# A DLRM tower on one core: handing over the x0b transfers one by one

## What is computed

```python
e = jnp.stack([tbl_0[ids[:, 0]], ..., tbl_31[ids[:, 31]]], axis=1)      # (1024, 32, 16)
xk = x0 = e
for W in (W0, W1, W2):                                                  # (32, h, 64)
    xk = relu(einsum('bmd,bhd,mhk->bkd', x0, xk, W))
    outs.append(sum(xk, axis=2))
h = concatenate(outs + [dense_ctx], axis=1)                             # (1024, 208)
h = relu(h @ W_top1 + b_top1); h = relu(h @ W_top2 + b_top2); y = h @ W_top3
```

## Time and profile before

| | |
|---|---|
| median of three runs | 791.03 us (784.43 to 791.82) |
| the profiled execution | 797.63 us |
| its span, first to last instruction | 795.8 us |
| mean granted TensorE clock in it | 0.953 |
| PE, DVE, POOL, ACT busy | 82%, 69%, 58%, 39% of the span |
| x0b: transfers, queue | 120 of 512 KB and 16 of 256 KB (block 0), SP |
| bytes moved | 121.57 MB, mean 153 GB/s |

### The profile page before, as it was taken

How to read it: one execution, slowest core, us unless ns; L and a number is a source line. 1 busy time by engine, 2 the same in 40 slices (tenths; PEclk the granted TensorE clock), 3 DMA queues, 4 the chain that set the end, 5 groups by cost and what they waited for, 6 DMA issues and landing times.

```text
span 795.8 us, 8373 instructions
## 1 busy us (share of the span) xinstructions
PE 656.4 (82%) x3096; PEld 268.9 (34%) x3096; DVE 551.6 (69%) x274; ACT 310.7 (39%) x586; POOL 464.6 (58%) x332
## 2 busy tenths in 40 slices
PE   0047798797989789897999799996988879999987
PEld 0012133233443334333443244433432334434435
DVE  1005796976939496796859496794939679798581
ACT  0004261616334171624535271714517072717131
POOL 6756687673838667358838667383956733335100
PEclk9999999898989899998999999899999999999998
DMA  7569749691983739663698749473793919872000
GB/s 182 125 185 229 207 137 212 177 208 37 259 237 72 147 116 224 183 144 75 183 205 212 141 139 229 156 160 58 212 229 100 199 46 255 216 168 45 0 1 0
DMA packets 59112, 121.57 MB, mean 153 GB/s; under 512 B 15369, under 2 KB 32017, under 8 KB 58977
## 3 DMA queue, kind: packets, MB, share of 16 engines
q1 hardware_dynamic: 40336, 112.41, 57.3%
q10 hardware_dynamic: 10544, 6.53, 2.8%
q0 software_dynamic: 8192, 2.11, 2.8%
HBM read 116.82 MB, written 5.25 MB: 153 GB/s over the span
## 4 chain that ended last, share of the span: by engine, by line
PE 47%; issue 15%; DVE 10%; ACT 9%; another core or an unknown queue 9%; POOL 9%; DMA 1%; DVEq 0%; ACTq 0%; POOLq 0%
PE acc L632 38%; DVE z_dve L373 9%; POOL emb L320 8%; ACT xq L449 4%; PE psm L701 3%; ACT xq L441 3%; PE psm L710 2%; PE acc L647 2%; ACT xs L441 1%; DMA emb<-in_tbl_dram,ids_cur 1%; PE psm L688 1%; POOL z_pool L329 1%; PE psm L678 1%; DVE zacc L398 0%
## 5 line engine op out<-in xcount | busy, mean ns | idle before, releaser
L373 DVE TENSOR_TENSOR z_dve<-xq,x0b 128x2048 f32<-128x2048 f32 x210 | 464.6, 2285 | 128.5 <-ACT xq L441 99.5
L632 PE MATMUL acc<-z_dve,w_cin 128*64 128x512 f32 x1680 | 393.5, 603 | 29.6 <-DVE z_dve L373 19.9
L329 POOL TENSOR_TENSOR z_pool<-x0b,xs 128x2048 f32<-128x2048 f32 x46 | 208.4, 4560 | 165.3 <-ACT xs L441 163.7
L320 POOL DMA_INDIRECT emb<-in_tbl_dram,ids_cur x256 | 246.7, 964 | 83.7 <-issue 80.2
L632 PEld LDWEIGHTS acc<-z_dve,w_cin 128*64 128x64 f32 x1680 | 119.6, 138 | 277.1 <-issue 206.4
L441 ACT ACTIVATE xq<-acc 64x512 f32<-64x512 f32 x128 | 73.0, 570 | 268.8 <-remote 151.7
L449 ACT ACTIVATE xq<-acc 32x512 f32<-32x512 f32 x256 | 144.4, 564 | 24.9 <-DVE z_dve L373 15.5
L373 DVE TENSOR_TENSOR z_dve<-xq,x_rot 128x2048 f32<-128x2048 f32 x30 | 68.0, 2292 | 41.1 <-PE acc L632 24.7
L632 PE MATMUL acc<-z_dve,w_sym 128*64 128x512 f32 x256 | 71.3, 639 | 19.0 <-issue 11.4
L632 PE MATMUL acc<-z_pool,w_cin 128*64 128x512 f32 x368 | 85.9, 602 | 0.0
L647 PE MATMUL acc<-z_extra,w_extra 128*64 128x128 f32 x256 | 31.0, 319 | 27.9 <-issue 25.7
(11 more groups left out here) (39 smaller groups left out, 188.6 us busy)
## 6 DMA issues: line engine op xcount, KB each, us to landing
x0b<-x0t SPq DMA_DIRECT2D x120, 512.0 KB
x_rot<-x0t SPq DMA_DIRECT2D x64, 512.0 KB
x_rep<-x0t SPq DMA_DIRECT2D x16, 512.0 KB
emb<-in_tbl_dram,ids_cur POOLq DMA_INDIRECT x256
x0b<-x0t SPq DMA_DIRECT2D x16, 256.0 KB
x0t<-emb_t ACTq DMA_DIRECT2D x14, 256.0 KB, 2.6
w_cin<-in_L_rec_W_dram SPq DMA_DIRECT2D x16, 64.0 KB
x_lo<-x0t SPq DMA_DIRECT2D x16, 64.0 KB
```

What stands on the lines that cost most here:

```text
L320: nc.gpsimd.indirect_dma_start(out=emb[:, D * f:D * f + D], out_offset=None, in_=tables[f], in_offset=bass.IndirectOffsetOnAxis(ap=ids_cur ...
L329: nc.gpsimd.tensor_tensor(z_pool[:, k % ZP_SLOTS, :, :], x0b[b % 2][:, 2 * j:2 * j + 2, :], xs[:, :].unsqueeze(1).broadcast_to([P, 2, N]), ...
L373: nc.vector.tensor_tensor(z_dve[:, k % Z_SLOTS, :, :], in0.unsqueeze(1).broadcast_to([P, 2, N]), in1, ALU.mult).then_inc(z_made, 1)
L632: ins = nc.tensor.matmul(acc[l][K * side:K * side + K, :], weights[c], z[:, c, NH * side:NH * side + NH], start=start and c == 0, stop=sto ...
```

## The change

The eight transfers of x0b(b+1) are no longer handed over together at the start of block b. The first four (first half) are issued one after the other, each behind a wait for one of the first four DVE products of L1(b). The last four (second half) stand behind `load_l0(b+2)` in SP's order, each behind a wait for one of the four NAT products of L2(b). Block 0's own loads, in groups of two chunks, stay as they were and only get a function of their own.

```diff
+            def load_x0b_group(g):
                 for r in range(4):
-                    sp.dma_start(x0b[b % 2][Q * r:Q * r + Q, c0:c1, :],
-                                 x0_rows(b, r + 4 * c0, [[0, Q], [4 * ROW, c1 - c0], [1, N]])
+                    sp.dma_start(x0b[0][Q * r:Q * r + Q, 2 * g:2 * g + 2, :],
+                                 x0_rows(0, r + 8 * g, [[0, Q], [4 * ROW, 2], [1, N]])
+                                 ).then_inc(x0b_in[0][g // 2], 16)
+
+            def load_x0b(b, c0, z_gates):
+
+                for r in range(4):
+                    sp.wait_ge(z_made, z_gates[r])
+                    sp.dma_start(x0b[b % 2][Q * r:Q * r + Q, c0:c0 + CH // 2, :],
+                                 x0_rows(b, r + 4 * c0, [[0, Q], [4 * ROW, CH // 2], [1, N]])
                                  ).then_inc(x0b_in[b % 2][c0 // (CH // 2)], 16)
...
-                load_x0b(0, 2 * g, 2 * g + 2)
+                load_x0b_group(g)
             for b in range(BLOCKS):
                 if b < LAST:
                     wait_x0t((b + 1) // 2)
                     if b > 0:
                         sp.wait_ge(z_made, l2_phase_end(b - 1, SWP))
                         sp.wait_ge(zp_made, zp_end(b - 1))
-                    load_x0b(b + 1, 0, CH // 2)
-                    load_x0b(b + 1, CH // 2, CH)
+                    load_x0b(b + 1, 0, [z_before[1, b, v, j] + 1 for v, j in l1_dve(b)[:4]])
...
                     sp.wait_ge(z_made, l0_end(b + 1))
                     sp.wait_ge(ze_made, b + 2)
                     load_l0(b + 2)
+                if b < LAST:
+                    load_x0b(b + 1, CH // 2, [z_before[2, b, NAT, j] + 1 for j in range(PAIRS)])
```

More of the change, by code:

```diff
@@ L248, in x0_rows @@
                 return bass.AP(x0t, t * (2 * M * ROW) + (row * ROW + s * N + col), dims)
-            def load_x0b(b, c0, c1):
+            def load_x0b_group(g):
                 for r in range(4):
-                    sp.dma_start(x0b[b % 2][Q * r:Q * r + Q, c0:c1, :],
-                                 x0_rows(b, r + 4 * c0, [[0, Q], [4 * ROW, c1 - c0], [1, N]])
+                    sp.dma_start(x0b[0][Q * r:Q * r + Q, 2 * g:2 * g + 2, :],
[6 more added lines that the diff above has]
+                                 x0_rows(b, r + 4 * c0, [[0, Q], [4 * ROW, CH // 2], [1, N]])
                                  ).then_inc(x0b_in[b % 2][c0 // (CH // 2)], 16)
```

## The result

| | before | after |
|---|---|---|
| median of four runs each | 791.42 us (784.43 to 796.93) | 899.09 us (895.82 to 899.92) |
| the profiled execution | 797.63 us | 895.82 us |
| its span | 795.8 us | 894.0 us |
| mean granted TensorE clock | 0.953 | 0.894 |

The changed kernel takes 1.135 times as long, with a 95% interval of 1.129 to 1.140. The forecast was 860 us, with a range of 828 to 888. The sign and the mechanism came as forecast, the size did not.

What follows compares the result with a forecast made beforehand. POOL's cycle (products, gathers, 2.8 us, ACT's copies) was taken as the bound. Six odd and five even blocks +62.0, then -4, +10.4 and +1: +69.4 on 797.63, 867.0 traced, 860.4 us as median, range 828 to 888.

Steps and rivals of the forecast that it cites:

- tile written after xs: Even blocks' `load_l0` waits for ACT's next tile, written 5.1 us after POOL begins the odd block's products.
- landing behind it: `load_l0` (12.5 us) and four late x0b transfers (10.1 us) land 22.6 us behind the written tile.
- third product to next xs: Odd blocks: POOL's third product 4.5, ids and gathers with z_extra 20.6, release 2.8, x1_pool 2.4 us.
- block 12: Even block after the summed eleven: 42 us in place of 46.0, so -4.
- block 13: Odd block without gathers: 5.1 + 22.6 + 4.5 + 8.8 for PE, then ACT's copies, 50.3 us, so +10.4.
- ahead of block 1: Block 0: `load_l0(1)` now stands behind four L1(0) products, put at 1 us (0 to 3).
- Rival A: 7%: PE's releases held from soon after the first gather; odd blocks 64.9 us, even blocks 46, about 926 us.
- B: 5%: DMA traffic holds PE and thinning it frees PE; even blocks 36.45 us, odd 50.3, about 781 us.
- C: 4%: the late half is absorbed, time within 1%, under 8 us in seven late blocks.
- the new even block: Even blocks with no late transfers: between 39.1 us (both ACT copies out of the chain) and 46.0, taken as 42.
- odd blocks, second half: Late x0b transfers issued in odd blocks, needed 9.1 us into POOL's next products: a few us of cover, cost nothing.
- the hold: PE's releases are held up while POOL issues gathers, and come out some 2.8 us behind the last one.

Runs made afterwards that it cites:

- waits alone: Kernel before with all eight waits, but the second half ahead of the tile's wait and of `load_l0`: 805.57 us, 1.011 of the kernel before.
- warm kernel: Changed kernel with twelve more 128x512 matmuls on PE in each odd block, after L1's third product: 846.25 us, 1.174 of the kernel before.
- the split: Kernel before with each block's second eight gathers held until PE releases L1(b): 744.09 us (0.923), then 740.39 (0.933) and 723.65 (1.007).

## Why the prediction was wrong, point by point

**The sum against the trace.** The traced time was to be 867.0 us and was 895.82. By the terms of the sum:

| term | forecast | measured | difference in all |
|---|---|---|---|
| tile written after xs, six odd blocks | 5.1 | 6.5 (5.1 to 8.8) | +8.6 |
| landing behind it | 22.6 | 23.3 (22.4 to 25.6) | +4.4 |
| third product to next xs | 30.3 | 30.4 | +0.4 |
| five even blocks, 2 to 10 | 42 | 44.1 (40.9 to 45.9) | +10.3 |
| block 12 | 42 | 46.7 | +4.7 |
| block 13 | 50.3 | 55.0 | +4.7 |
| ahead of block 1 (+1 forecast) and at the end | | | -4.3 |

That is +28.8 us, all of the miss of the traced time. The six even blocks are 15.0 of them. The median misses by 9.9 us more: I took off 6.6 us because the profiled execution of the kernel before was that much above its median, and the profiled one of after is 3.3 us below its own. That the offset would carry over was assumed.

**Right: what bounds, who waits, and where.** The third POOL product waits alone in blocks 1, 3, ... 13, for 18.4 to 24.5 us; the late transfers stand back to back behind `load_l0`; the odd blocks are 58 to 64 us; x2_nat and x2_swp run inside the burst there. The first half's waits cost nothing that can be told (waits alone, 1.011). Rival A's 65 us for the odd blocks didn't come (block 7's 64.2 us have a late tile and a landing of 25.6 us in them, and both copies ran inside the burst), nor B's 36 us for the even ones; C's absorption didn't either.

**The step that failed: the new even block.** It was put between 39.1 and 46.0 us, and I took 42, "nearer the middle", from no row; it measured 44.5 in the mean of six. With 42 in all six the median would have come out at 884 us, inside the range. Two things were left out of it, and the second is the larger.

Block 4 shows the first. Its 43.1 us are 9.1 of two products, 4.0 of waiting for x0b, 4.6 for the third, 20.2 from its end to the last gather's, and 5.2 to xs: the lower end of 39.1, plus the 4.0 us of a cover called sufficient in the part on odd blocks. The forecast costed "odd blocks, second half" at nothing and never asked what the even block would be with it. Block 12 has 0.9 us of this, the others none. Block 6's 44.6 us have another wait in them, 6.04 us behind POOL's first gather, which the kernel before has as well.

The second is the hold. In blocks 8, 10 and 12 (45.9, 45.9 and 46.7 us) no gain is left, and they are 12.4 of the 15.0 us. The changed kernel at the end of block 10, PE, POOL's last gather, ACT, and POOL's next products:

```profile
604.41 7.04 PE L641 MATMUL acc<-z_dve,w_cin 128*64 128x512 f32 x32
...
614.77 0.94 POOL L329 DMA_INDIRECT emb<-in_tbl_dram,ids_cur  x1 [0.31 <-issue]
...
618.34 2.31 ACT L450 ACTIVATE xq<-acc 64x512 f32<-64x512 f32 x4 [14.30 <-remote]
...
627.78 4.56 POOL L338 TENSOR_TENSOR z_pool<-x0b,xs 128x2048 f32<-128x2048 f32 x1 [12.06 <-ACT xs L450]
```

PE's L1 is over at 611.45 and x2_nat comes at 618.34, 6.9 us later and behind the last gather, with 12.06 us of POOL's idle time, as in the earlier trace rows. L1 ended 14 to 16 us into the burst in blocks 8, 10 and 12, and 11 us into it in blocks 2 and 4, which kept their gain. At the lower level, where nothing is held, blocks 2, 4, 8, 10 and 12 of the changed kernel all take 37.9 to 39.3 us. So in half of the even blocks it was rival A's even half that came, without its odd half. The two had been tied into one rival, though they are decided separately. Why L1 is later in blocks 8, 10 and 12 than in 2 and 4 stays open.

**A term mis-sized: the written tile.** 5.1 us was the interval of one pair of blocks. It was 5.1, 6.9, 8.8, 7.9, 5.5, 5.1 and 5.1 us in the seven. In block 4 ACT's last copy of the tile waited for PE:

```profile
312.02 0.59 ACT L529 COPY emb_t<-psm 128x512 f32<-128x512 f32 x1 [3.71 <-PE psm L687]
```

That the lateness of one pair is handed on to the next through PE is argued from this row, not shown by a run. The landing was sized nearly rightly from the rows, 23.3 us against 22.6. The fit of the Trainium skill ("SBUF — State Buffer", "The DMA setup-cost knee", with "Door 1: The DMA port swizzle"), which gave an estimate of 17.9 us, is further off; here the measurement decides.

**A term left out: PE's clock, in block 13.** The stretches of the changed kernel around block 5's gap (busy us of PE, PEld, DVE, ACT, POOL, then granted clock, DMA share, GB/s), and PE's rows there:

```profile
322.00:332.00 10.00, 9.61 (x42) 5.44 (x40) 0.85 (x1) 1.74 (x5) 0.00 (x0) 1.00 1.03 230
332.00:343.00 11.00, 0.00 (x0) 0.00 (x0) 4.35 (x2) 0.00 (x0) 4.30 (x1) 0.67 0.96 209
343.00:347.00 4.00, 3.74 (x10) 1.25 (x12) 4.00 (x4) 1.11 (x2) 3.12 (x5) 0.50 0.90 188
...
329.72 1.89 PE L641 MATMUL acc<-z_dve,w_cin 128*64 128x512 f32 x8
343.26 3.68 PE L641 MATMUL acc<-z_pool,w_cin 128*64 128x512 f32 x8 [11.65 <-POOL z_pool L338]
```

While PE stood for 11.65 us its granted clock fell from 1.00 to 0.50, from 2.4 to 1.2 GHz, and its next eight matmuls took 3.68 us in place of 1.89. The Trainium skill's page "TensorE: Matmul & The Clock Gate" (Part 1, on the clock gate) gives these two levels and says that an idle engine drops to the lower one; the trace agrees. In block 5 nobody waits for that: xs there hangs on the gathers. In block 13 there are none, PE's five products took 11.4 us and not 8.8, and that is some 2.6 of its 4.7 us (the landing's 24.5 us are another 1.9). The warm kernel says the same at the lower level. Its rows of PE in block 5, and then in block 15:

```profile
316.94 10.57 PE L758 MATMUL psm<-wt_a,ident 128*128 128x512 f32 x24
328.43 1.94 PE L642 MATMUL acc<-z_pool,w_cin 128*64 128x512 f32 x8 [0.92 <-POOL z_pool L339]
...
787.39 10.57 PE L758 MATMUL psm<-wt_a,ident 128*128 128x512 f32 x24
```

In block 5 PE is at full speed behind the gap. Yet the kernel's ratio of 1.174 (1.163 to 1.185) is no better than the unwarmed one's 1.167, and that is misleading: block 15 is odd too, but has no gap, and there the 10.57 us of extra matmuls stand in PE's way. From the start of block 15's products to the end the warm kernel takes 79.7 us, the unwarmed one 69.1. Up to there, from block 1 on, it takes 659.6 us against 661.3. So warming gained some 2 us in fourteen blocks, by one trace of each kernel; their runs spread by more (842 to 850 and 835 to 841 us). Block 13 is shorter, 51.4 against 54.3 us, and blocks 3, 5 and 7 by 1 to 3 us, but blocks 4 and 12 are 3 to 5 us longer.

**What the hold had to do with it.** At the lower level the changed kernel's chain is the same, only with nothing held. POOL in block 5 of the changed kernel there:

```profile
294.12 9.04 POOL L338 TENSOR_TENSOR z_pool<-x0b,xs 128x2048 f32<-128x2048 f32 x2
324.01 4.51 POOL L338 TENSOR_TENSOR z_pool<-x0b,xs 128x2048 f32<-128x2048 f32 x1 [20.85 <-DMA x0b<-x0t]
...
349.08 4.57 POOL L338 TENSOR_TENSOR z_pool<-x0b,xs 128x2048 f32<-128x2048 f32 x1
```

55.0 us for the odd block, where POOL goes from its last gather to the next product with no idle time; the kernel before takes 39.9 there. So the same change costs 121 us at the lower level (718 to 840) and 107 at the upper (in the two comparisons there, 791 to 899 and 798 to 905). By my reading, a kernel that already waits has some of the new wait for free. In the runs without gathers the difference of the spans was 94 us; the rest of the 121 us comes with the gathers, which stand behind the late third product on POOL.

## What to carry to other kernels

In a queue that issues in order, look at what each transfer is moved behind, and at what that one waits for: the waits that the change is named for cost 1% at most, and the place in the queue over 12%. Before a difference of 1% is given a cause, run the unchanged kernel once more beside itself: here that gave 1.011. If an edit is costed at nothing because of cover, put the cover's size in us beside it, and carry its shortfall into the block in which it would come out. If engines stand still while one of them issues a long run of small indirect DMAs, run the kernel once without them; here one wait that broke the run in two gave 7 to 8% where the hold was there, and cost 0.7% where it was not. A filler put in to keep an engine busy in a gap must be kept out of the blocks that have no gap.

## What the runs showed of the hardware that was not expected

- While POOL issues 16 gathers, one each 1.25 us, PE's releases can reach the other engines 9.5 us late, behind the last one. What PE finished 10 to 11.4 us into the burst came out inside it in the changed kernel's odd blocks, 1.9 to 3.1 us late. PE starts small matmuls 1.83 us apart then. An eighth of x0b's bytes changes nothing in it (ratio 1.008), leaving the gathers out ends it (0.881 and 0.888), and a pause of 2.77 us in them lets the releases out (0.923 and 0.933).
- The hold is not there in each comparison. The same kernel took 791 to 801 us in four comparisons (the first one among them) and 718 in two, steadily within each. The record numbers the chips of the five comparisons 8, 0, 0, 11 and 7, so that number 0 stands once beside 800 us and once beside 718: if it is the same chip both times, the chip alone does not decide. What does stays open, and the traces don't name the mechanism. The split in the changed kernel was not run at the upper level.
- Removing the hold from the kernel before by the split is worth 56 and 57 us at one level and loses 5 at the other. So where the level is unknown, the kernel before with the split is the one to take by these runs: 740 to 744 and 724 us, against 798 to 801 and 718.
